# Value matmuls of a cross attention in two groups of six chunks a unit instead of three of four

## The reference, cut to what matters

```python
scores = jnp.einsum('bqhd,bkhd->bhqk', Q, Kp) / jnp.sqrt(jnp.float32(HD))
a = jax.nn.softmax(scores, axis=-1)
o = jnp.einsum('bhqk,bkhd->bqhd', a, V).reshape(Bq, Sq, Dm)
return o @ wo + bo
```

## Time and profile before

| | us |
|---|---|
| median of 3 runs (lowest, highest) | 585.22 (582.52, 587.19) |
| the profiled execution | 585.68 |
| its span, first to last instruction | 583.9 |
| PE busy / DVE / ACT / POOL | 519.4 / 418.8 / 363.4 / 206.0 |
| granted TensorE clock, mean over the span | 0.933 |

### The profile page before, as it was taken

One profiled execution on the slowest core, in us unless ns is written; L12 is line 12 of the kernel. 1 busy time (PEld: TensorE's weight loads), 2 busy tenths in 40 slices (PEclk: granted clock), 3 DMA queues, 4 the chain that ended last, 5 costly groups with the idle time before them and its releaser, 6 DMA issues.

```text
span 583.9 us, 17011 instructions
## 1 busy us (share of the span) xinstructions
PE 519.4 (89%) x6536; PEld 380.2 (65%) x6536; DVE 418.8 (72%) x818; ACT 363.4 (62%) x716; POOL 206.0 (35%) x357
## 2 busy tenths in 40 slices
PE   6889789999999999998779995699999999999984
PEld 4766456676767677676557774367676776767763
DVE  7799877777787778786353115868879788878753
ACT  2456457677777767777534431477777677776663
POOL 7543323031221327363123001337365474530101
PEclk9788759999999999999959997679999999999998
DMA  6427379567557373746502220266574734538000
GB/s 155 108 82 223 108 227 271 151 198 191 177 138 213 132 196 124 198 146 159 161 0 72 72 74 0 59 193 184 135 218 156 179 147 131 170 68 232 10 2 18
DMA packets 41116, 79.99 MB, mean 137 GB/s; under 512 B 9326, under 2 KB 19246, under 8 KB 41054
## 3 DMA queue, kind: packets, MB, share of 16 engines
q1 hardware_dynamic: 41054, 79.16, 47.5%
HBM read 58.95 MB, written 20.13 MB: 135 GB/s over the span
## 4 chain that ended last, share of the span: by engine, by line
PE 66%; DVE 12%; ACT 8%; issue 7%; DMA 3%; POOL 2%; SPq 1%; ACTq 1%; POOLq 0%; DVEq 0%
PE bank L442 13%; PE bank L420 12%; PE bank L408 11%; PE bank L376 6%; PE bank L1302 5%; PE bank L370 4%; PE bank L1291 4%; PE bank L364 3%; ACT qfix L539 2%; DMA k_scratch<-kparts 2%; ACT scratch L562 2%; PE bank L382 2%; ACT kparts L546 1%; DVE weights L1490 1%; DVE mx L609 1%
## 5 line engine op out<-in xcount | busy, mean ns | idle before, releaser
L609 DVE TENSOR_REDUCE mx<-bank 112x1 f32<-112x500 f32 x384 | 245.9, 673 | 52.3 <-PE bank L408 48.9
L562 ACT ACTIVATE scratch<-bank 125x448 f32<-125x448 f32 x384 | 203.6, 548 | 106.2 <-PE bank L420 104.4
L408 PE MATMUL bank<-krep,qfix 96*112 96x500 bf16 (+1 forms) x384 | 153.5, 410 | 3.8 <-ACT qfix L1011 1.4
L420 PEld LDWEIGHTS bank<-qfix,krep 99*128 99x128 bf16 (+1 forms) x1536 | 107.3, 100 | 73.1 <-issue 25.5
L420 PE MATMUL bank<-qfix,krep 99*128 99x112 bf16 (+1 forms) x1536 | 139.9, 215 | 15.4 <-ACT qfix L539 10.1
L442 PE MATMUL bank<-scratch,v 125*32 125x112 f32 x3072 | 94.0, 262 | 0.0
L442 PEld LDWEIGHTS bank<-scratch,v 125*32 125x32 f32 x3072 | 70.2, 109 | 9.2 <-ACT scratch L562 0.6
L735 POOL TENSOR_TENSOR oT<-comb,rec 128x56 f32<-128x56 f32 x32 | 9.8, 305 | 176.3 <-DVE rec L631 176.3
L724 POOL TENSOR_TENSOR kparts<-k_rest,kparts 128x500 bf16<-128x500 f32 x48 | 54.3, 1139 | 44.9 <-ACT kparts L546 44.6
L408 PEld LDWEIGHTS bank<-krep,qfix 96*112 96x112 bf16 (+1 forms) x384 | 51.6, 136 | 27.0 <-issue 19.6
L1302 PEld LDWEIGHTS bank<-scratch 128*112 128x112 f32 x256 | 32.7, 181 | 16.0 <-issue 10.7
(11 more groups left out here) (172 smaller groups left out, 698.5 us busy)
## 6 DMA issues: line engine op xcount, KB each, us to landing
krep<-k_scratch SPq DMA_DIRECT2D x192, 187.5 KB, 4.1
k_scratch<-kparts SPq DMA_DIRECT2D x16, 1125.0 KB, 4.5
ctx_tile<-in_ctx SPq DMA_DIRECT2D x16, 750.0 KB
scratch<-in_L_xattn_e_w SPq DMA_DIRECT2D x16, 256.0 KB, 3.1
Q<-q_scratch SPq DMA_DIRECT2D x12, 168.0 KB, 3.1
q_scratch<-scratch SPq DMA_DIRECT2D x6, 168.0 KB, 2.5
Q<-q_scratch SPq DMA_DIRECT2D x12, 56.0 KB, 2.2
k_rest<-in_selq SPq DMA_DIRECT2D x1, 576.0 KB, 11.9
```

What stands on the lines that cost most here:

```text
L408: nc.tensor.matmul(row_bank(v, c, lead)[0:PQ, 0:KB], qfix[0:KR[l], slot, p * PQ:(p + 1) * PQ], krep[0:KR[l], slot, p, n * KB:(n + 1) * KB] ...
L420: ins = nc.tensor.matmul(SCORES[c % 2][:, p * PQ:(p + 1) * PQ], krep[0:KS[l], slot, p, c * KP:c * KP + 128], qfix[0:KS[l], slot, p * PQ:(p ...
L562: nc.scalar.activation(P[:, p_slot(s_, slot), :], SCORES[slot % 2][0:KP, 0:UQ], ACT.Exp, scale=SCALE).then_inc(z["exp_ok"], 1)
L609: nc.vector.tensor_reduce(mx[:, par, c // NKB, c % NKB:c % NKB + 1], row_bank(v, c, lead)[0:PQ, 0:KB], AX.X, ALU.max).then_inc(z["row_max" ...
```

## The change

PBUF goes from 8 to 12, and PV runs in two groups of six chunks a unit: chunks 6 to 11 of the unit before behind slot 1, chunks 0 to 5 behind slot 7. The P buffers lie in `scratch`, which grows to 3840 + 12 x 448 = 9216 floats a partition; `weights` and `v_all` lose their own tensors and are placed in `scratch`, where the self attention leaves room.

```diff
--- before.py
+++ after.py
@@ -37,7 +37,7 @@
 VROW = 160
 SCALE = float(HD) ** -0.5
 CREDIT = 1
-PBUF = 8
+PBUF = 12
 PV_CREDIT = PBUF
 BIG = 1e30
 NEG = -1e30
@@ -174,7 +174,7 @@
         mask_row = sq[0:B, :, :].rearrange("p c d -> p (c d)").bitcast(BF16)[:, 0:SK]
 
 
-        SCR = 7424
+        SCR = 3840 + PBUF * UQ
         scratch = sb("scratch", [128, SCR])
 
         qbd = scratch[:, 0:1792].rearrange("p (r h q) -> p r h q", r=2, h=H)
@@ -198,9 +198,9 @@
         P = scratch[0:KP, 3840:3840 + PBUF * UQ].rearrange("p (r n) -> p r n", r=PBUF)
         hid = scratch[:, 5632:5632 + 4 * TOK].rearrange("p (r n) -> p r n", r=4)
         gateT = kT[0:E, :]
-        v_all = sb("v_all", [S, B, 128])
         WT = 7 * S + 128 - S
-        weights = sb("weights", [128, 2, WT])
+        weights = scratch[:, 6448:6448 + 2 * WT].rearrange("p (r n) -> p r n", r=2)
+        v_all = scratch[0:S, 7376:7376 + B * 128].rearrange("p (b d) -> p b d", b=B)
         logit = sb("logit", [TP, TT, E])
         prob = sb("prob", [TP, TT, E])
         one1 = sb("one1", [TP, TT, E])
@@ -443,9 +443,9 @@
                                        P[:, p_slot(s_, c), g * PQ:(g + 1) * PQ], start=(c == 0), stop=(c == KC - 1))
             ins.then_inc(z["pv_ok"], 1)
 
-        def pe_pv_four(pe, l, j, s_, first):
-
-            for c in range(first, first + 4):
+        def pe_pv_six(pe, l, j, s_, first):
+
+            for c in range(first, first + 6):
                 pe_pv(pe, l, j, s_, c)
 
         def pe_attend(pe, l, among):
@@ -483,13 +483,13 @@
                         pe_st(pe, l, u, s_, slot)
 
                         if slot == 1 and s_ > 0:
-                            pe_pv_four(pe, l, j, s_ - 1, 8)
+                            pe_pv_six(pe, l, j, s_ - 1, 6)
                         if slot == 1 and s_ == 0 and not begins(j):
-                            pe_pv_four(pe, l, j - 1, 3, 8)
-                        if slot in (5, 9):
-                            pe_pv_four(pe, l, j, s_, slot - 5)
+                            pe_pv_six(pe, l, j - 1, 3, 6)
+                        if slot == 7:
+                            pe_pv_six(pe, l, j, s_, 0)
                     if last and s_ == 3:
-                        pe_pv_four(pe, l, j, s_, 8)
+                        pe_pv_six(pe, l, j, s_, 6)
                     for item in got.get(13, []):
                         pe_item(pe, item, base + k, order_[k])
                         k += 1
```

## The result

| | before | after |
|---|---|---|
| median, us (lowest, highest) | 584.99 (582.52, 587.19) | 604.62 (602.24, 606.91) |
| the profiled execution | 585.68 | 606.91 |
| its span | 583.9 | 605.1 |
| granted clock, mean | 0.933 | 0.935 |

The changed kernel is slower: the ratio is 1.0315, 95% interval 1.0272 to 1.0359, four executions of each. The forecast was 598.0; the time lies in the upper part of its range.

What follows compares the result with a forecast made beforehand. PE's own instruction order bounds the attentions, except where PE waits for ScalarE. K units +12.7, V units +1.1, first K units -0.7, DMA wait -0.7: +12.4 us, forecast 598 us, range 589 to 606.

Steps and rivals of the forecast that it cites:

- K unit: Unit with three transposes and three key projections: 14.46 us against 13.40, +1.06 in each of 12.
- V unit: Unit with three groups of value projections: 12.14 us against 12.07, +0.07 in each of 15.
- K1 is held by the residual: K unit: second key projection waits for VectorE's residual of the first, 3.01 us after it; PE idle at least 1.04.
- ACT's chain ends the unit: From slot 8's ST to the next unit's first ST ScalarE decides: 3.51 us in K, 3.02 in V units.
- the waits of the ST of slots 11 and 0 in a K unit: PE's waits there for ScalarE's exponential and maxima copy: 1.5 us together.
- The price of a group: Value matmuls on PE: 0.31 us fixed plus 0.183 a chunk; a group of four 1.04, of six 1.41.
- Rival C: Nothing about a group of value matmuls is fixed, each six costs 1.56 us: +8.4, 606.0 us; chance 0.08.
- Rival A: Removed drains decide, ScalarE keeps up wherever groups stand, PE saves 9.8 us: 575.4 us; chance 0.08.
- rival B: K units: K1 is held less than reckoned since K0's high copy comes sooner; a wash, 585.2 us; chance 0.10.
- the tail of each layer: Two more chunks behind the last ST can run under the last exponential: nothing, at most +0.4 us each.
- The DMA wait of the second K unit: First layer: PE's 0.99 us wait for a DMA of keys, about 0.7 us of it won back.
- the first K units: First K unit of each layer, without D, where K1 doesn't wait: -0.35 us each, -0.7 for the two.

Runs made afterwards that it cites:

- e2: Changed kernel with item D of the K units in slot 3 instead of 5, so K1 takes another bank: 594.15 us, ratio 1.0133.
- e4: Changed kernel with ScalarE's middle part of K1 behind the exponential of slot 7 instead of 8: 596.14 us, ratio 1.0159.
- e6: Kernel before with ScalarE's copy of the maxima (M) ahead of the exponential of slot 10 instead of behind it: 577.76 us, ratio 0.9801.
- e5: Kernel before with four groups of three chunks a unit, behind slots 1, 4, 7 and 10: 598.38 us, ratio 1.0209.
- e1: Changed kernel, keeping twelve P buffers and the scratch placement, but with groups of four behind slots 1, 5, 9 again: 586.53 us, ratio 1.0015.
- e7: Changed kernel with the second group behind slot 9, D of K units in slot 3, and the M copy ahead of slot 10's exponential: 579.45 us, ratio 0.9887.
- e10: Changed kernel with VectorE's copy of the next queries (L601) in V units behind slot 7's maximum instead of slot 8's: 600.78 us, ratio 1.0255.
- e3: Changed kernel with the second group of six behind slot 9 instead of 7: 593.73 us, ratio 1.0167.
- e9: The changed kernel run once more, nothing altered: 604.91 us, ratio 1.0314.
- e11: Changed kernel with only ScalarE's M copy moved ahead of the exponential of slot 10: 610.19 us, ratio 1.0404.
- e8: Changed kernel with ScalarE's high copy of a K item ahead of the exponential of its slot instead of behind it: 596.04 us, ratio 1.0163.

## Why the prediction was right in its kind, and what its sum lacked

**The units: right.** K unit, predicted 14.46, measured 14.45 in the one shown and 14.37 to 14.45 in the undisturbed ones of layer two; its parts 3.92, 3.01, 4.02, 3.51 came out as 3.94, 3.01, 4.03, 3.47. V unit, predicted 12.14 (9.12 and 3.02), measured 12.05 for most (9.14 and 2.91 in the one behind the K unit shown) and 12.13 to 12.27 for the others: +0.06 against those before for most. That K1 is held by the residual is shown by e2, which takes that hold away; that ACT's chain ends the unit by e4, and for the order of the kernel before by e6. Two of its signs came out smaller: the waits of the ST of slots 11 and 0 in a K unit are 1.10 us together where 1.5 was said, and PE's busy time fell by 3.0 us over the whole kernel where up to 10 was said for the attentions (its idle time rose by 24.2, as forecast). PE's rows hide short waits: in the V unit behind the one shown the ST of slot 7 comes 0.59 us after the ST ahead of it (469.57 to 470.16) where a bare slot takes 0.41, and its row shows no idle time.

**The price of a group: right.** Six chunks span 1.36 us where 1.34 was said; from the ST ahead of the group to the row behind it are 1.57 us (457.60 to 459.17) against 1.20 for four (e6), and 1.01 for three (449.78 to 450.79 in e5), so two chunks more than four cost the 0.37 that were reckoned, and six cost 1.41. Rival C (1.56 for six) falls. Rival A (the drains decide, 575.4) and rival B (K1 hardly held) fall by the times themselves and by the rows of K1, e1 and e2. A was right of one thing: with the holds removed, groups of six do reach 579 (e7). But so do groups of four.

**The size: missed by 6.6 us** (604.6 against 598.0), within the range. The weak step is the list of exceptions, in which everything outside ordinary units was set at nothing or as a gain. What the runs showed in its place:

- The last unit of the first layer, put down under "the tail of each layer, at most +0.4". It has neither row matmuls nor much else for PE to do, so the waits for exponentials lie bare in it. In e10, against 11.31 us before (276.73 to D at 288.04), it took 12.97:

```profile
291.88 0.37 PE L420 MATMUL bank<-qfix,krep 99*128 99x112 bf16 x4 [0.44 <-ACT scratch L562]
292.80 0.37 PE L420 MATMUL bank<-qfix,krep 99*128 99x112 bf16 x4 [0.55 <-ACT scratch L562]
293.11 1.36 PE L442 MATMUL bank<-scratch,v 125*32 125x112 f32 x48
295.34 0.40 PE L387 MATMUL bank<-comb,cst 128*128 128x56 f32 x2 [0.88 <-DVE comb L624]
```

  That is +1.7 of the +2.3 to +3.0 us between the layers' units (107.22 in e10, 107.84 after, 104.89 before). With the group at slot 9 most of it is gone (11.63 in e3). The tail of the second layer grew by 0.5 us, just over its bound of 0.4.
- The last K unit of the first layer: 15.90 against 14.54, +1.36 where +1.06 was reckoned (14.54 in e1 too).
- The collision of the copy with the squares, +1.2 us, placed (e9, e10). It was no term.
- The DMA wait of the second K unit, "about 0.7 won back": not in the profile after (a wait of 0.9, the unit 15.56), but in e9 and e10 (no wait, 14.63). In the kernel before it comes and goes too (14.34 there, 13.59 in e1). So it varies between executions, and the 0.7 can't be told from that.
- In the other direction, the first K units are 0.68 and 1.38 us shorter than in the profile before, together 1.4 more than the 0.7 reckoned. These two vary in any kernel (in e1, in the order of the kernel before, they take 14.25 and 12.96 where the kernel before has 13.72 and 14.06), so nothing follows for the term.
- Not placed, in the profiled execution: two falls of the clock. The V unit at 151 us took 13.64 instead of 12.05, the K unit at 220 us 16.22 instead of 14.64: 3.2 us together. Ahead of the fall at 152 PE was busy 1.53 of 2 us, among waits for K1 and for exponentials. e9 shows that the time stays at 604 to 605 without them, so they are no part of the mean loss that can be named. The fall at 220 began 0.7 us behind the end of PE's wait of 1.11 us for the collision, and those of e4 and e11 near there 0.6 and 0.9 us behind the same wait; but e2, e8 and e9 have that wait and no fall. Whether the wait helps to bring it is open.

For e9, whose clock does not fall in the first 14 units, the account closes: to the profile before (585.68) it is 18.2 us longer; +9.2 in the first 15 units (of it 5.2 in five ordinary K units, 2.7 in the last K unit, 1.2 the collision, -0.7 the first unit, and 0.8 in the second K unit and the other V units), +2.6 between the layers, +4.3 in the second layer, 1.5 and 0.5 at the two ends, and 0.1 outside the span. Layer one's last K unit is 17.20 in e9 against 15.90 after, and this too is the clock: it is at the lower level from 284.66 to 288.08 us, and the 12 matmuls at the end of that unit take 2.90 us where they take 1.56 in the profile after. First e9, then after:

```profile
284.75 2.90 PE L1056 MATMUL bank<-wo,oT 128*112 128x128 f32 x12 [0.89 <-DVE oT L1067]
```

```profile
288.81 1.56 PE L1056 MATMUL bank<-wo,oT 128*112 128x128 f32 x12 [0.89 <-DVE oT L1067]
```

Set against the 12.4 us of the forecast, e9's excess of 5.8 us is: 2.6 between the layers, 1.6 in the last K unit (1.3 of it this fall of the clock), 1.5 ahead of the first unit (scatter, see e1), 1.2 the collision, and 0.3 in the rest, less 1.4 in the first K units.

## What to carry to other kernels

A block of work on a busy engine has a place as well as a price: here two of the three groups of four each covered work of ScalarE that PE needs next, and two groups of six, 0.3 us cheaper a unit, left both bare, for 1.4 us more of waits in a K unit. Find the chain that ends each part of a loop and reckon it as starts of one row to starts of the next; five such sums gave the unit to 0.1 us, while sums over shares of busy time said the opposite. Reckon the first, the last and the boundary unit of a loop in the same way, since they have less work to hide a wait, and before larger blocks are tried look for an engine's idle gap beside the instruction that others wait for: moving one copy into it won 2% (e6), and the same edit lost where there was no gap (e11).

## What the hardware showed that had not been expected

A DVE copy of 100x448 in bf16 takes 0.27 us; beside GpSimd's tensor_tensor of 125x1536 it took 2.84, when it began 0.04 us after it, and 0.27 when it began 0.6 us or more ahead. Every one of the 35 long copies ended 0.13 us after the instruction of GpSimd under which it began, a short one of 0.2 us or a long one of 2.75. Three copies that began within 0.004 us of one took 0.27, and there GpSimd's instruction took 0.33 instead of 0.21. Four maxima (L609) out of PSUM ran beside the same squares in e10 in 2.61 us, 0.65 each, as ever. That fits the Trainium skill ("Trainium Architecture — The Big Picture", What this means for kernel authors), which says that DVE and GpSimd share a pair of ports as an exclusive lock and do not split its bandwidth. Here the copy came 0.9 us later against the squares (from 0.86 ahead to 0.04 behind), and that cost PE 1.2 us, in one of 30 copies.

The granted clock of PE fell to the lower level for 3 to 4 us in the middle of an attention in which PE was busy nine tenths of the time. Between 92 and 280 us such falls came in the profiles of after (two), e4 and e11, and in e7 behind a DMA wait of 1.7 us, and not in those of the kernel before, e1, e2, e3, e5, e6, e8, e9 and e10; the two units that met one in the profile after were 1.6 us longer. With the same program they came twice in one execution (after) and not at all between 92 and 280 us in another (e9).
